# Moving the apply step of Q and K, and half of the V casts, in a fused transformer layer

## The chip, the cores and the metric

The kernel runs on the 8 cores of one Trainium2 chip. Each core computes one of the eight sequences of the batch (2048 tokens, 1024 features) on its own; the cores exchange nothing. The metric is the device time of the slowest core in microseconds.

## What is computed

One layer: a layer norm, then the sum of the input, an attention block with its own MLP, and a mixture of eight experts. The change touches the projections of Q, K and V and the normalisation of Q and K per head. Cut to that:

```python
xn = _rms_norm(x, ln1_w)                       # x: [B, 2048, 1024]
q = (xn @ Wq).reshape(B, S, HEADS, HEAD_DIM)   # 16 heads of 64
k = (xn @ Wk).reshape(B, S, HEADS, HEAD_DIM)
v = (xn @ Wv).reshape(B, S, HEADS, HEAD_DIM)
q = _normalize_kq(q)     # kq * rsqrt(sum(kq^2 over the head) + 1e-6)
k = _normalize_kq(k)
...
attn = softmax(causal(scale * (q @ k^T + bias)))
y = attn @ v @ Wo + x ; MLP(rms_norm(y)) + y
```

## The kernel before

The kernel works feature-major: a tile holds 128 features (two heads) on the partitions and all T = 2048 tokens in the free dimension, so NP = T // 512 = 4 pieces of 512 columns, and NTT = T // 128 = 16 tiles of tokens. There are eight feature tiles, counted by d. The stages are: layer norm and transposes, gating, experts (to about 790 us), RMS norm and the Wq projections (to about 867 us), the Wk projections with the normalisation of Q, the Wv projections with the normalisation of K, attention, Wo, and the MLP.

Instructions are written by hand with the helper `kb.op(engine, fn, reads, writes)`. Each engine runs its own in the order in which they are written. The helper derives semaphore waits from the names in `reads` and `writes`: a reader waits for the last writer of the name, a writer for the last writer and all readers since. A name stands for a whole tile (or PSUM bank `pb0` to `pb7`), never for a part of it; for an engine's semaphore the wait is for its count at the last such instruction.

The parts that matter here:

- `proj_unit` (L744 to 773): a unit of 8 x 4 = 32 matmuls (L755) into banks 0 to 3, then four casts on VectorE (L770) to the Q or K tile. It first issues the eight loads of the next weight tile from POOL.
- `qn_sq` (L775): the square of a Q or K tile on VectorE, 128 x 2048 (L778).
- `qn_stats` (L782 to 805): for each of four pieces a matmul that sums the squares per head (L787), then Ln and Exp on ScalarE (L792, L796) through one scratch row, and for Q a multiply by the scale on VectorE (L801). The result is `rowb16`, one name per parity of d.
- `qn_apply_piece` (L807 to 818): a matmul that spreads one piece of `rowb16` over 128 partitions (L810), and a multiply on VectorE into the Q or K tile (L815).
- `v_transpose` (L834 to 845): a transpose of 128 x 128 of V on TensorE into bank 4 (L837), and two casts of 64 columns each out of the bank into `VtL` (L843), one for each head. Both casts write the name `vtl{tt}`, and the next transpose writes the name `pb4`, which both read.

The loop over d for Wk (L823 to 830) writes: square of Q d, projection of K d, statistics of Q d, apply of Q d-1. The apply of Q 7 follows (L831). The loop for Wv (L847 to 875) writes: square of K d, loads, for each k of 0 to 7 four projection matmuls (L858), two transposes of V d-1 and, at odd k, one apply piece of K d-1 in bank 7, then four copies of V d (L872) and the statistics of K d. Sixteen transposes of V 7 and four apply pieces of K 7 end the stretch (L876 to 879).

Of the kernel before, what the change touches and what calls it, by code (L numbers as in the profile page):

```python
# [194 lines left out]
def build_nc(T=2048):  # L195
    nc = bass.Bass("TRN2", target_bir_lowering=False)
    NTT = T // 128
    NP = T // 512
# [15 lines left out]
    kb = KB(nc)  # L214
# [6 lines left out]
    pb = [None] * 8  # L221
# [36 lines left out]
    def ld(dst, src, cast=False, sem=MISC, reads=(), writes=(), silent=False,  # L258
# [15 lines left out]
       writes=("ln1b",))  # L274
    ld(ln2b[:, :], A(w_d["ln2"], 0, [[D, 1], [1, D]]), cast=True, sem="qC",
       writes=("ln2b",))
    for e_ in range(NTRU):
        ld(ebCol[:, e_ * 8:(e_ + 1) * 8], A(w_d["eb"], e_ * D, [[1, 128], [128, 8]]),
           writes=("ebCol",), slow=True)

    G, V, S, TE = "gpsimd", "vector", "scalar", "tensor"
# [462 lines left out]
    def proj_unit(wname, dst, dkey, dout, nxt):  # L744
        def go():
            par = dout % 2
            if nxt is not None:
                wload(1 - par, w_d[nxt[0]], 0, nxt[1] * 128,
                      (nxt[1] + 1) * 128, f"wst{1 - par}")
            pbase = (dout % 2) * 2 if NP <= 2 else 0  # L750
            for k in range(8):
                for pp in range(NP):
                    bk = pbase + pp if NP <= 2 else pp
                    kb.op(TE, lambda e, par=par, k=k, pp=pp, bk=bk:
                          e.matmul(pb[bk][:, 0:512],  # L755
                                   Wst[par][:, k * 128:(k + 1) * 128],
                                   XN2[k][:, pp * 512:(pp + 1) * 512],
                                   start=(k == 0), stop=(k == 7)),
                          reads=(f"wst{par}", f"y16p_{k}"),
                          writes=(f"pb{bk}",), inc=(k == 7))  # L760
            for pp in range(NP):
                bk = (pbase + pp) if NP <= 2 else pp
                if dst is None:
                    kb.op(V, lambda e, pp=pp, bk=bk:
                          e.tensor_copy(Vf32[:, pp * 512:(pp + 1) * 512],
                                        pb[bk][:, 0:512]),
                          reads=(f"pb{bk}",), writes=("vf32",))
                else:
                    kb.op(V, lambda e, dout=dout, pp=pp, bk=bk:
                          e.tensor_copy(dst[dout][:, pp * 512:(pp + 1) * 512],  # L770
                                        pb[bk][:, 0:512]),
                          reads=(f"pb{bk}",), writes=(dkey.format(dout),))
        return go
# [8 lines left out]
    def qn_stats(XB, keyfmt, c, fold_scale, bank0):  # L782
        pr = c % 2
        for pp in range(NP):
            bk = bank0 + pp % 2
            kb.op(TE, lambda e, pr=pr, pp=pp, bk=bk:
                  e.matmul(pb[bk][0:2, 0:512], selq[:, :],  # L787
                           sqP[pr][:, pp * 512:(pp + 1) * 512],
                           start=True, stop=True),
                  reads=(f"sq{pr}", "selq"), writes=(f"pb{bk}",))  # L790
            kb.op(S, lambda e, bk=bk:
                  e.activation(rowscrP[0:2, :], pb[bk][0:2, 0:512], AF.Ln,  # L792
                               bias=epsc[0:2, 2:3]),
                  reads=(f"pb{bk}", "epsc"), writes=("rowscrP",))
            kb.op(S, lambda e, pr=pr, pp=pp:
                  e.activation(rowb16[pr][0:2, pp * 512:(pp + 1) * 512],  # L796
                               rowscrP[0:2, :], AF.Exp, scale=-0.5),
                  reads=("rowscrP",), writes=(f"rowb16_{pr}",))
            if fold_scale:
                kb.op(V, lambda e, c=c, pr=pr, pp=pp:  # L800
                      e.tensor_scalar(rowb16[pr][0:2, pp * 512:(pp + 1) * 512],  # L801
                                      rowb16[pr][0:2, pp * 512:(pp + 1) * 512],
                                      scaleP[:, c:c + 1], None, ALU.mult),
                      reads=(f"rowb16_{pr}", "scaleP"),
                      writes=(f"rowb16_{pr}",))
# [17 lines left out]
    for d in range(8):  # L823
        nxt = ("Wk", d + 1) if d < 7 else ("Wv", 0)
        qn_sq(Q16, "q16_{}", d)
        proj_unit("Wk", K16, "k16_{}", d, nxt)()
        qn_stats(Q16, "q16_{}", d, True, 4)
        if d > 0:
            for pp in range(NP):
                qn_apply_piece(Q16, "q16_{}", d - 1, pp, 6 + pp % 2)  # L830
    for pp in range(NP):  # L831
        qn_apply_piece(Q16, "q16_{}", 7, pp, 6 + pp % 2)

    def v_transpose(c, tt):  # L834
        reg = (tt % 4) * 128
        kb.op(TE, lambda e, tt=tt, reg=reg:
              e.transpose(pb[4][:, reg:reg + 128],  # L837
                          Vf32[:, tt * 128:(tt + 1) * 128], iden_f[:, :]),
              reads=("vf32", "iden_f"), writes=("pb4",))
        for hf, eng in ((0, V), (1, V)):  # L840
            hh = 2 * c + hf
            kb.op(eng, lambda e, tt=tt, reg=reg, hf=hf, hh=hh:
                  e.tensor_copy(VtL[tt][:, hh * 65:hh * 65 + 64],  # L843
                                pb[4][:, reg + hf * 64:reg + hf * 64 + 64]),
                  reads=("pb4",), writes=(f"vtl{tt}",))

    for d in range(8):  # L847
        par = d % 2
        qn_sq(K16, "k16_{}", d)
        if d < 7:  # L850
            wload(1 - par, w_d["Wv"], 0, (d + 1) * 128, (d + 2) * 128,
                  f"wst{1 - par}")
        pbase = (d % 2) * 2 if NP <= 2 else 0
        for k in range(8):
            for pp in range(NP):
                bk = pbase + pp if NP <= 2 else pp
                kb.op(TE, lambda e, par=par, k=k, pp=pp, bk=bk:
                      e.matmul(pb[bk][:, 0:512],  # L858
                               Wst[par][:, k * 128:(k + 1) * 128],
                               XN2[k][:, pp * 512:(pp + 1) * 512],  # L860
                               start=(k == 0), stop=(k == 7)),
                      reads=(f"wst{par}", f"y16p_{k}"),
                      writes=(f"pb{bk}",), inc=(k == 7))
            if d > 0 and 2 * k < NTT:
                v_transpose(d - 1, 2 * k)
                v_transpose(d - 1, 2 * k + 1)
            if d > 0 and k % 2 == 1 and (k - 1) // 2 < NP:
                qn_apply_piece(K16, "k16_{}", d - 1, (k - 1) // 2, 7)
        for pp in range(NP):
            bk = pbase + pp if NP <= 2 else pp  # L870
            kb.op(V, lambda e, pp=pp, bk=bk:
                  e.tensor_copy(Vf32[:, pp * 512:(pp + 1) * 512],  # L872
                                pb[bk][:, 0:512]),
                  reads=(f"pb{bk}",), writes=("vf32",))
        qn_stats(K16, "k16_{}", d, False, 5)
# [462 lines left out]
```

## Time and profile before

| | us |
|---|---|
| median of 3 runs (2912.61 to 2984.51) | 2916.29 |
| the profiled execution | 2929.51 |
| its span on the slowest core, number 2 | 2927.9 |
| spans of the eight cores | 2897.7 to 2927.9 |
| TensorE busy | 2174.8 (74%) |
| VectorE busy | 1037.4 (35%) |
| ScalarE busy | 605.7 (21%) |
| GpSimd busy | 660.4 (23%) |

The span runs from the first to the last instruction of a core; the execution's own time has 1.6 us around it. Busy shares are averages over all stages. Matmuls overlap each other, so the duration of one is longer than its share of a dense stream: a 512-column matmul in such a stream starts about 0.22 us after the one before it when the granted clock is 2.4 GHz and about 0.43 us when it is 1.2 GHz. The mean granted clock over the execution is 0.765 of full.

### The profile page before, as it was taken

Reading aid. Unit: us, or ns where it says so; the run is one execution under the profiler, and the core shown is the slowest. Engines: PE = TensorE matmul, PEld = TensorE weight load, DVE = VectorE, ACT = ScalarE, POOL = GpSimd, SP = SyncE. Lnnn points to the kernel's source line nnn. Section 1 sums busy time; section 2 is a strip of 40 time slices with the busy share of each in tenths; the row PEclk is TensorE's granted clock in tenths of the full one; section 3 lists DMA queues with packets and bytes.
Section 4 is the critical chain, followed back from the end, with each engine's and each line's share of the span. In section 5 each row is a group of like instructions: output and inputs, shape, how many; then the busy total and the mean of one; then the engine's idle time right before and its main releaser. Section 6 shows DMA issues by size and latency. Waiting matters only on the chain.

```text
span 2927.9 us, 28314 instructions; the slowest of 8 cores (2897.7 to 2927.9 us)
## 1 busy us (share of the span) xinstructions
PE 2174.8 (74%) x7379; PEld 745.0 (25%) x7379; DVE 1037.4 (35%) x2125; ACT 605.7 (21%) x1204; POOL 660.4 (23%) x764
## 2 busy tenths in 40 slices
PE   2457999998686677768889898865369989988322
PEld 0212444443132222212222222221013323332111
DVE  3725444443434444445555555532320000000111
ACT  1400000000003211126665666610002101210000
POOL 0021478776142211000000000013135302410000
PEclk9987999999597755555655655667569999999655
DMA  2202323233121100001100111025168513421343
GB/s 42 80 1 29 44 29 44 29 44 121 19 27 17 14 8 8 4 15 19 19 15 11 19 19 19 12 62 129 72 92 112 91 48 68 54 47 58 105 130 124
DMA packets 137150, 139.20 MB, mean 48 GB/s; under 512 B 46320, under 2 KB 116976, under 8 KB 133882
## 3 DMA queue, kind: packets, MB, share of 16 engines
q0 software_dynamic: 96320, 61.39, 16.2%
q1 hardware_dynamic: 40682, 76.00, 8.2%
q8 instruction: 73, 1.20, 0.2%
q14 instruction: 75, 0.61, 0.1%
HBM read 160.80 MB, written 33.69 MB: 66 GB/s over the span
## 4 chain that ended last, share of the span: by engine, by line
PE 64%; DVE 10%; issue 9%; DMA 8%; ACT 5%; POOL 2%; SPq 1%; DVEq 1%; ACTq 0%; POOLq 0%
PE pb L627 8%; PE pb L1199 8%; PE pb L973 7%; PE s L1029 7%; PE pb L755 4%; PE pb L858 4%; DMA asl<-accscr 3%; PE pb4b L1218 3%; DMA accw<-accscr 2%; PE pb7b L1218 2%; PE pb5b L627 2%; PE pb4b L627 2%; PE pb6b L627 2%; PE pb7b L627 2%; ACT pt L1036 2%
## 5 line engine op out<-in xcount | busy, mean ns | idle before, releaser
L1036 ACT ACTIVATE pt<-s 128x512 bf16<-128x512 f32 (+3 forms) x640 | 306.8, 533 | 270.5 <-PE s L1029 243.4
L1040 DVE TENSOR_TENSOR pt<-pt,tst 128x512 bf16<-128x512 bf16 (+3 forms) x640 | 238.3, 383 | 247.5 <-ACT pt L1036 233.4
L660 POOL TENSOR_TENSOR acc<-acc,mtmp 128x2048 f32<-128x2048 f32 x56 | 253.6, 4529 | 102.9 <-DVE mtmp L650 102.9
L1029 PE MATMUL s<-q,k 64*128 64x512 bf16 (+3 forms) x640 | 272.1, 525 | 0.9 <-ACT pt L1036 0.2
L973 PE MATMUL pb<-pt,vtl 128*65 128x512 bf16 (+3 forms) x640 | 262.3, 528 | 10.0 <-DVE pt L1040 0.4
L1199 PE MATMUL pb<-k,ws 128*128 128x512 bf16 x1024 | 241.3, 384 | 31.7 <-DMA ws<-W 22.2
L627 PE MATMUL pb<-xn,we 128*128 128x512 bf16 x1024 | 233.4, 381 | 5.2 <-DVE cwb L600 0.4
L264 POOL DMA_DIRECT2D ws<-W x264 | 139.9, 572 | 324.1 <-PE pb L1199 260.9
L1240 DVE TENSOR_TENSOR acw<-acw,pb4b 128x512 f32<-128x512 f32 x8 | 5.5, 689 | 559.8 <-PE pb7b L1218 379.5
L1199 PEld LDWEIGHTS pb<-k,ws 128*128 128x128 bf16 x1024 | 100.7, 99 | 173.1 <-issue 69.1
L264 POOL DMA_DIRECT2D tst<-cscr x16 | 8.6, 540 | 603.0 <-DVE pt L1040 507.4
L1297 PE MATMUL pb6b<-iden_f,asl 128*128 128x128 f32 x64 | 28.6, 447 | 148.0 <-DMA asl<-accscr 128.4
L755 PE MATMUL pb<-y16p,wst 128*128 128x512 bf16 x480 | 127.8, 417 | 12.7 <-DVE q L770 9.9
L627 PEld LDWEIGHTS pb<-xn,we 128*128 128x128 bf16 x1024 | 98.3, 98 | 135.3 <-issue 23.2
L1209 ACT ACTIVATE h<-pb 128x512 bf16<-128x512 f32 x96 | 57.3, 597 | 345.7 <-PE pb L1199 293.1
L650 DVE SCALAR_TENSOR_TENSOR mtmp<-pb,ebCol,cwb 128x512 f32<-128x512 f32 x112 | 84.1, 751 | 117.4 <-PE pb L627 108.6
L973 PEld LDWEIGHTS pb<-pt,vtl 128*65 128x65 bf16 x640 | 80.7, 148 | 150.2 <-issue 143.3
L858 PE MATMUL pb<-y16p,wst 128*128 128x512 bf16 x256 | 113.5, 599 | 0.1
L710 ACT ACTIVATE rowscrP<-pb4b,epsc 1x512 f32<-1x512 f32 x1 | 0.7, 677 | 535.0 <-PE pb6b L704 535.0
L843 DVE CAST vtl<-pb4b 128x64 bf16<-128x64 f32 x256 | 57.9, 226 | 142.7 <-PE pb4b L837 129.1
L1029 PEld LDWEIGHTS s<-q,k 64*128 64x128 bf16 x640 | 52.8, 107 | 207.1 <-issue 203.8
L837 PE MATMUL pb4b<-iden_f,vf 128*128 128x128 f32 x128 | 55.1, 431 | 65.8 <-DVE vtl L843 65.7
(263 smaller groups left out, 2877.7 us busy)
## 6 DMA issues: line engine op xcount, KB each, us to landing
ws<-W POOLq DMA_DIRECT2D x264, 64.0 KB, 2.6
we<-ew POOLq DMA_DIRECT2D x128, 128.0 KB, 5.4
xt<-x SPq DMA_DIRECT2D x16, 512.0 KB, 3.5
accscr<-acc SPq DMA_DIRECT2D x8, 1024.0 KB, 3.8
tst<-cscr POOLq DMA_DIRECT2D x16, 512.0 KB, 5.5
accw<-accscr SPq DMA_DIRECT2D x8, 1024.0 KB, 8.0
accscr<-accw SPq DMA_DIRECT2D x8, 1024.0 KB, 5.0
acw<-accscr SPq DMA_DIRECT2D x16, 512.0 KB, 5.0
```

Of the source, the lines that this page charges most:

```text
L264: e.dma_start(d, s, allow_slow_non_contiguous=sl),
L627: e.matmul(pb[bk][:, 0:512], We16[par][:, k * 512 + col: k * 512 + col + 128], XN16[k][:, pp * 512:(pp + 1) * 512], start=(k == 0), stop=( ...
L650: e.scalar_tensor_tensor(mtmp[mp][:, pp * 512:(pp + 1) * 512], pb[bk][:, 0:512], ebCol[:, e_ * 8 + dout:e_ * 8 + dout + 1], cwbA[e_][:, pp ...
L660: e.tensor_tensor(ACC[dout][:, :], ACC[dout][:, :], mtmp[mp][:, :], ALU.add),
L755: e.matmul(pb[bk][:, 0:512], Wst[par][:, k * 128:(k + 1) * 128], XN2[k][:, pp * 512:(pp + 1) * 512], start=(k == 0), stop=(k == 7)),
L858: e.matmul(pb[bk][:, 0:512], Wst[par][:, k * 128:(k + 1) * 128], XN2[k][:, pp * 512:(pp + 1) * 512], start=(k == 0), stop=(k == 7)),
L973: e.matmul(pb[b][0:65, q % 512:q % 512 + w], VtL[kt][:, h * 65:(h + 1) * 65], Pt[pslot][:, j0:j0 + w], start=(kt == 0), stop=lb),
L1029: e.matmul(s16[sbk][:, 0:w], K16[c][po:po + 64, kt * 128:(kt + 1) * 128], Q16[c][po:po + 64, q:q + w], start=True, stop=True),
L1036: e.activation(Pt[pslot][:, jc:jc + w2], s16[sbk][:, 0:w2], AF.Exp),
L1040: e.tensor_tensor(Pt[pslot][:, jc:jc + w2], Pt[pslot][:, jc:jc + w2], Tst[par][:, jc:jc + w2], ALU.mult),
L1199: e.matmul(pb[pbase + pc][:, 0:512], Wst1[par][:, k * 256 + hl * 128: k * 256 + hl * 128 + 128], YN16[k][:, t0c + pc * 512: t0c + (pc + 1) ...
L1218: e.matmul(pb[bk][:, 0:512], W2R[:, hk * D + dout * 128: hk * D + (dout + 1) * 128], H16[hk][:, pc * 512:(pc + 1) * 512], start=(hk == 0), ...
```

## The change

Three edits. In the Wk loop the apply of Q d-1 is written ahead of the projection of K d instead of behind the statistics of Q d. In `v_transpose` the second cast becomes a copy on ScalarE; both still write `vtl{tt}`. In the Wv loop the apply pieces of K d-1 go to k = 0, 1, 2, 3 instead of k = 1, 3, 5, 7.

```diff
     for d in range(8):
         nxt = ("Wk", d + 1) if d < 7 else ("Wv", 0)
         qn_sq(Q16, "q16_{}", d)
-        proj_unit("Wk", K16, "k16_{}", d, nxt)()
-        qn_stats(Q16, "q16_{}", d, True, 4)
         if d > 0:
             for pp in range(NP):
                 qn_apply_piece(Q16, "q16_{}", d - 1, pp, 6 + pp % 2)
+        proj_unit("Wk", K16, "k16_{}", d, nxt)()
+        qn_stats(Q16, "q16_{}", d, True, 4)
     for pp in range(NP):
         qn_apply_piece(Q16, "q16_{}", 7, pp, 6 + pp % 2)
...
-        for hf, eng in ((0, V), (1, V)):
+        for hf in range(2):
             hh = 2 * c + hf
-            kb.op(eng, lambda e, tt=tt, reg=reg, hf=hf, hh=hh:
-                  e.tensor_copy(VtL[tt][:, hh * 65:hh * 65 + 64],
-                                pb[4][:, reg + hf * 64:reg + hf * 64 + 64]),
-                  reads=("pb4",), writes=(f"vtl{tt}",))
+            if hf == 0:
+                kb.op(V, lambda e, tt=tt, reg=reg, hh=hh:
+                      e.tensor_copy(VtL[tt][:, hh * 65:hh * 65 + 64],
+                                    pb[4][:, reg:reg + 64]),
+                      reads=("pb4",), writes=(f"vtl{tt}",))
+            else:
+                kb.op(S, lambda e, tt=tt, reg=reg, hh=hh:
+                      e.copy(VtL[tt][:, hh * 65:hh * 65 + 64],
+                             pb[4][:, reg + 64:reg + 128]),
+                      reads=("pb4",), writes=(f"vtl{tt}",))
...
-            if d > 0 and k % 2 == 1 and (k - 1) // 2 < NP:
-                qn_apply_piece(K16, "k16_{}", d - 1, (k - 1) // 2, 7)
+            if d > 0 and k < NP:
+                qn_apply_piece(K16, "k16_{}", d - 1, k, 7)
```

## Rows read from the trace of the kernel before

**Rows 1.** Page, part 4: the chain that ended last, by engine.
```profile
PE 64%; DVE 10%; issue 9%; DMA 8%; ACT 5%; POOL 2%; SPq 1%; DVEq 1%; ACTq 0%; POOLq 0%
```
**Rows 2.** Windows, Wv stretch: length, busy of PE, PEld, DVE, ACT, POOL, clock, DMA, GB/s.
```profile
1010.40:1248.10 237.70, 173.52 (x429) 56.02 (x429) 100.73 (x294) 39.17 (x60) 25.41 (x48) 0.53 0.07 7
```
**Rows 3.** Timeline, Wk units 0 and 1: start, duration, engine, line, operation [idle before].
```profile
877.71 0.38 PE L787 MATMUL pb5b<-sq,selq 128*2 128x512 bf16 x1 [1.11 <-ACT rowscrP L792]
878.02 7.39 PE L755 MATMUL pb<-y16p,wst 128*128 128x512 bf16 x32
...
885.34 0.38 PE L787 MATMUL pb4b<-sq,selq 128*2 128x512 bf16 x1
```
**Rows 4.** Timeline, from the statistics of unit 1 to those of unit 2.
```profile
888.18 0.38 PE L787 MATMUL pb5b<-sq,selq 128*2 128x512 bf16 x1 [1.11 <-ACT rowscrP L792]
...
892.01 0.34 DVE L801 TENSOR_SCALAR rowb<-rowb,scaleP 2x512 bf16<-2x512 bf16 x1 [1.21 <-ACT rowb L796]
892.28 0.67 DVE L815 TENSOR_TENSOR q<-q,pb6b 128x512 bf16<-128x512 bf16 x1
...
893.20 0.58 PE L810 MATMUL pb6b<-rowb,sel2T 2*128 2x512 bf16 x1 [4.11 <-DVE q L815]
...
894.58 7.98 PE L755 MATMUL pb<-y16p,wst 128*128 128x512 bf16 x29
...
895.45 1.22 DVE L778 TENSOR_TENSOR sq<-q 128x2048 bf16<-128x2048 bf16 x1
...
903.44 0.38 PE L787 MATMUL pb4b<-sq,selq 128*2 128x512 bf16 x1
```
**Rows 5.** Timeline, unit 7 of Wk and the start of Wv.
```profile
987.70 10.15 PE L755 MATMUL pb<-y16p,wst 128*128 128x512 bf16 x32
...
997.77 0.38 PE L787 MATMUL pb4b<-sq,selq 128*2 128x512 bf16 x1
...
1000.62 0.38 PE L787 MATMUL pb5b<-sq,selq 128*2 128x512 bf16 x1 [1.11 <-ACT rowscrP L792]
...
1010.45 9.03 PE L858 MATMUL pb<-y16p,wst 128*128 128x512 bf16 x32
```
**Rows 6.** Timeline, two k steps of a Wv unit, the first with an apply piece.
```profile
1059.37 0.45 PE L837 MATMUL pb4b<-iden_f,vf 128*128 128x128 f32 x1 [0.91 <-DVE vtl L843]
...
1060.28 1.89 PE L858 MATMUL pb<-y16p,wst 128*128 128x512 bf16 x4
...
1061.96 0.42 PE L837 MATMUL pb4b<-iden_f,vf 128*128 128x128 f32 x1
1062.49 0.55 DVE L843 CAST vtl<-pb4b 128x64 bf16<-128x64 f32 x2 [1.34 <-PE pb4b L837]
...
1063.29 0.45 PE L837 MATMUL pb4b<-iden_f,vf 128*128 128x128 f32 x1 [0.91 <-DVE vtl L843]
...
1063.53 1.91 PE L858 MATMUL pb<-y16p,wst 128*128 128x512 bf16 x4
```
**Rows 7.** Timeline of the first stage: hand-overs between ScalarE, TensorE and VectorE.
```profile
59.97 0.27 ACT L424 COPY xnf<-pb6b 128x128 f32<-128x128 f32 x1 [0.45 <-PE pb6b L420]
...
60.38 0.45 PE L420 MATMUL pb6b<-iden_f,xnt 128*128 128x128 f32 x1 [0.27 <-ACT xnf L424]
...
62.02 0.21 DVE L399 TENSOR_SCALAR st_s<-st_s 128x1 f32<-128x1 f32 x1
62.33 0.29 ACT L404 ACTIVATE st_s<-st_s,epsc 128x1 f32<-128x1 f32 x1 [0.91 <-DVE st_s L399]
```
**Rows 8.** Timeline, start of a Wv unit: ScalarE's last step and T2.
```profile
1087.91 0.63 ACT L796 ACTIVATE rowb<-rowscrP 2x512 bf16<-2x512 f32 x1
...
1088.51 0.45 PE L837 MATMUL pb4b<-iden_f,vf 128*128 128x128 f32 x1 [0.92 <-DVE vtl L843]
```
**Rows 9.** Timeline, start of the tail of sixteen transposes: the second one, and ScalarE.
```profile
1249.46 0.45 PE L837 MATMUL pb4b<-iden_f,vf 128*128 128x128 f32 x1 [0.91 <-DVE vtl L843]
...
1250.37 0.63 ACT L796 ACTIVATE rowb<-rowscrP 2x512 bf16<-2x512 f32 x1
```

## Prediction of the time after the change

> **What bounds the kernel now.** I read the page first. The chain of work that ended last is TensorE for 64% and VectorE for 10% [rows 1], so time is won or lost where TensorE waits. The edits lie between about 867 and 1277 us: the Wk projections with the normalisation of Q, then the Wv projections with the transposes of V and the normalisation of K. The windows view shows the second stretch: 237.70 us, TensorE busy for 173.52, ScalarE for only 39.17, at a mean granted clock of 0.53, which is almost wholly the 1.2 GHz level [rows 2]. So one engine is full but slow, ScalarE has room, and every step is short. Then I read the timeline around one unit of each kind, looking for what released TensorE.
>
> In the Wk stretch a unit is 32 matmuls, then four statistics matmuls paced by ScalarE, then four pieces of "apply". Unit 1 follows unit 0's statistics at once: last statistics matmul at 877.71, projection from 878.02 to the next statistics at 885.34, so a gap of 0.31 and 7.32 us of projection at 2.4 GHz [rows 3]. From unit 2 on the apply of the unit before stands in between: last statistics matmul 888.18, next projection 894.58, a gap of 6.40 [rows 4]. There are six such gaps, 6.38 to 6.42 each. TensorE is idle there for 4.11 us until VectorE has finished its multiply at 892.28, and that multiply stands behind the last L801 at 892.01, although its own data are long ready: the queue, not the data, makes it late. TensorE comes out of the gap at 1.2 GHz. Unit 2 needs 903.44 - 894.58 = 8.86 us, unit 7 needs 997.77 - 987.70 = 10.07 [rows 4, 5]; these are the first and last of six that alternate between about 8.9 and 10.0, so the mean is 9.47. After the last unit two rounds of apply follow each other: 1000.62 to 1010.45, a gap of 9.83 [rows 5].
>
> In the Wv stretch each of eight k steps is four matmuls (1060.28 to 1061.96, 1.68 us, 0.42 each, the 1.2 GHz level), a transpose T1, two casts one after the other on VectorE, and a transpose T2 that must wait for both: 1061.96 to 1063.29, 1.33 us. T2 to the next matmuls is 0.24 us without an apply piece and 1060.28 - 1059.37 = 0.91 with one [rows 6].
>
> **The change, part by part.**
>
> *Apply moved ahead of the projection.* In each of d = 1 to 7 the apply of d-1 now follows that unit's own statistics directly. Those data are not ready yet. Its first matmul reads rowb16, whose last writer is the fourth L801, ending at 892.01 + 0.34 = 892.35. VectorE to TensorE takes 893.20 - (892.28 + 0.67) = 0.25, so the matmul would start at 892.60 and, at 1.2 GHz (0.58, as at 893.20), be readable near 893.28. In VectorE's queue the square of Q (L778, 1.22 us) now stands in front of the multiplies: 892.28 + 1.22 less the overlap of 0.05 gives 893.45. The later of the two, 893.45, replaces 892.28: every following step is 1.17 later, and the gap becomes 6.40 + 1.17 = 7.57 [rows 4]. Behind the last unit there is no square and only one round: 6.40 + 1.00 = 7.40.
> Before: 0.31 + 6 x 6.40 + 9.83 = 48.5 us. After: 7 x 7.57 + 7.40 = 60.4. That is +11.9.
> Unit 1 loses its seamless start, so it should be paced like the others: 9.47 - 7.32 = +2.15. Sum for the stretch: +14.0. No transfer is issued in another order, since each weight load of POOL waits for the projection before it and takes its place as before.
>
> *Half of each V cast on ScalarE.* Both copies name the same tile vtl as written, so the ScalarE copy waits for the VectorE cast as well as for the transpose. They run one after the other as before, not side by side. The new chain is T1 to the cast 0.53, the cast 0.23, the hand-over to ScalarE 62.33 - (62.02 + 0.21) = 0.10, the copy, and ScalarE to TensorE 60.38 - (59.97 + 0.27) = 0.14 [rows 6, 7]. No row has a 64-column copy. The bound above is the 128-column one, 0.27. Below, ScalarE's Exp over 512 columns takes 0.63 [rows 8] against 0.27 for 128 [rows 7], 0.36 / 384 = 0.94 ns a column, so 0.27 - 0.06 = 0.21; that is the form nearest to it and I take it. The chain is 0.53 + 0.23 + 0.10 + 0.21 + 0.14 = 1.21 against 1.33: 0.12 less. If both hand-overs took the 0.25 of VectorE to TensorE and the copy 0.27 it would be 1.53: 0.20 more. I take 1.21, since two of the three parts are rows of the very same engines.
> The ScalarE page of the Trainium skill ("ScalarE: Activation LUTs", What ACT_TABLE_LOAD costs) gives 186 ns plus 0.833 ns a column with immediate scale and bias, 293 ns for 128 columns, where the trace has 0.27 us; for 64 columns it would say 239 ns and the gain would be 0.09 a step instead of 0.12, about 2 us in all.
>
> *What ScalarE has queued in front.* At the start of a Wv unit ScalarE still works on K's statistics: its last step ends at 1087.91 + 0.63 = 1088.54. The first copy of a unit waits for it, so T2 comes at 1088.54 + 0.21 + 0.14 = 1088.89 instead of 1088.51: +0.38 [rows 8].
>
> *K's pieces at k = 0 to 3 instead of 1, 3, 5, 7.* Each costs 0.91 - 0.24 = 0.67 in its place. The one that leaves k = 7 was followed by the statistics, 0.13 cheaper. The piece at k = 0 needs rowb16, complete at 1088.54, before T2: no new stall. In exchange the copies of V out of the banks are free some 0.6 earlier, which nobody waits for.
>
> Each of seven units: 7 x (-0.12) + 0.38 + 0.13 = -0.33, so -2.3. In the tail sixteen transposes run as a bare chain. The second now waits until ScalarE is free at 1250.37 + 0.63 = 1251.00, and starts at 1251.35, not 1249.46: +1.9 [rows 9]. Fourteen more steps at -0.12 give -1.7. The tail is +0.2.
>
> **Sum.** 14.0 - 2.3 + 0.2 = +11.9 us. Against the profiled execution's 2929.5 that is 2941.4; the median of the runs shown is 13.2 lower, 2916.3, and there the forecast is 2928.2. Whatever lies behind 1277 us is shifted and not changed.
>
> **The rivals.**
>
> *A, slower than before by over 2%: the hand-overs are dear.* Place: T1, cast, copy, T2, 56 times in the loop and 15 times in the tail. With the upper bound of 1.53 the loop and the tail cost 71 x 0.32 = 23 us more than forecast, 2951. To pass 2% (58 us above 2916, so 46 above the forecast) each chain must take 0.65 more, 1.86 in all. For it: the copy waits for TensorE and VectorE, and the next transpose for VectorE and ScalarE, two waits where there was one. Against it: no hand-over in the rows is above 0.25.
> The trace page of the Trainium skill ("Perfetto Trace Analysis", Identifying Dependency Chains) says that an instruction which waits on several engines may get extra semaphore instructions put in front of it, which speaks for A; no row of before shows what such an instruction costs here.
>
> *B, the clock stays at 1.2 GHz through the Wk units.* The gap of 7.57 has only four short matmuls in it. At 0.42 a unit takes 13.4 instead of 9.47: 7 x 3.9, and 4.4 for the first Wv unit, which now takes about 9.0 [rows 5]: +32, 2960. Against it: TensorE is dense for 32 matmuls, and after gaps of 6.40 and of 9.83 the level came back each time.
>
> *C, the Wv steps gain the 2.4 GHz level.* Steps 4 to 7 have no pieces now: four in a row of 1.68 + 1.21 + 0.24 = 3.1 us, with nothing between the steps. At 7.32 / 32 = 0.23 a matmul, a step is 0.76 shorter; over 28 steps 21 us, 2907. It puts the kernel ahead of before from 16 such steps on. Against it: the loop fell to 1.2 GHz and stayed there, though half of its steps had no piece either, and its mean was 0.53 [rows 2].
>
> *D, the moved apply does not cool TensorE,* because the gap is cut up in another way than before: the 2.15 of each of seven units comes back, -15 against the forecast, 2913. Against it: the idle part of the gap is as long as before, 888.56 to 892.60.
>
> **How the numbers follow.** Forecast 0.70, A 0.08 (of which 0.02 past 2%), B 0.07, C 0.08, D 0.07. The forecast is that of the first. Its own range is 2920 to 2940, from the unit pace (7.32 to 10.07 for unit 1) and the copy. To hold 8 in 10 with the upper bound of A, I take 2913 to 2950. A measurement tells 2% from no change here, 58 us; only the far end of A reaches it, with 0.02, and 0.01 more for A and B together; on the other side none of the cases does, and 0.01 is left for C with more steps than priced: slower 0.03, faster 0.01, same 0.96.
>
> **What the profile after would show.** Right: seven gaps near 7.6 from last statistics to projection, one near 7.4; L778 between the last L801 and the first L815 of a unit; unit 1 taking 8.9 to 10.0; T1 to T2 near 1.21 in the loop and in the tail; the ScalarE copy starting only after the VectorE cast has ended, and the first of a unit after K's last Exp; the granted clock of the Wv stretch still near 0.5. Wrong: a copy beside the cast, a chain above 1.4, a Wv stretch with a clock clearly above 0.53, or a Wk unit of 13 us.

## The result, and the profile after

The changed kernel takes 2944.0 us (median of 10 runs), the kernel before 2919.2 (median of 10, with the three shown above). The ratio is 1.0084, 95% interval 1.0071 to 1.0096: +0.84%, +24.5 us. The forecast was 2928.2, +11.9. So the sign, the verdict (within 2%) and the range of 2913 to 2950 held; the forecast case's own range, 2920 to 2940, did not, and the size was about half of what came.

The profiled execution of after took 2942.17 us, its slowest core 2940.6, again number 2. Some executions of either kernel run with one die at a lower clock; the ratios leave them out.

The whole of the difference has to be found between the first statistics matmul of unit 0 and the first matmul of attention, since nothing else was edited. Read from the timelines of all cores (core 2; the others agree within 0.4, except core 5, which has 137.1 and 150.7 in the first line and 265.8 before in the second):

| stretch | before | after | forecast |
|---|---|---|---|
| Wk: first statistics matmul to first Wv projection | 135.6 | 153.7 | +14.0 |
| Wv: to the first matmul after the last memset | 266.6 | 269.6 | -2.1 |
| sums of V and first tile of the bias, to attention | 19.6 | 20.7 | 0 |
| together | 421.8 | 444.0 | +11.9 |

That is +22.2 of the 24.5 us. The other 2 us are not located: attention (638.3 to 650.9 us on the eight cores before, 639.2 to 649.5 after), Wo (197.1 to 216.1 and 197.6 to 203.9) and the MLP (766.4 to 769.9 and 767.1 to 774.7) scatter by more than that.

The chain that ended last looks as before: TensorE 64% and VectorE 10% as in [rows 1], ScalarE 6% where it had 5%.

Timeline of after, from the last statistics matmul of unit 0 to the first of unit 1, to be laid beside [rows 3, 4]:
```profile
876.24 0.38 PE L787 MATMUL pb5b<-sq,selq 128*2 128x512 bf16 x1 [1.12 <-ACT rowscrP L792]
...
880.06 0.34 DVE L801 TENSOR_SCALAR rowb<-rowb,scaleP 2x512 bf16<-2x512 bf16 x1 [1.20 <-ACT rowb L796]
880.33 1.21 DVE L778 TENSOR_TENSOR sq<-q 128x2048 bf16<-128x2048 bf16 x1
...
880.55 0.58 PE L810 MATMUL pb6b<-rowb,sel2T 2*128 2x512 bf16 x1 [3.94 <-DVE rowb L801]
...
881.47 0.67 DVE L815 TENSOR_TENSOR q<-q,pb6b 128x512 bf16<-128x512 bf16 x1
...
883.76 10.19 PE L755 MATMUL pb<-y16p,wst 128*128 128x512 bf16 x32
...
893.88 0.38 PE L787 MATMUL pb4b<-sq,selq 128*2 128x512 bf16 x1
```
The order is the forecast one: last L801, square, multiply. TensorE waits 3.94 us for `rowb16`; the gap is 883.76 - 876.24 = 7.52 us where unit 1 had 0.31; and the projection behind it takes 893.88 - 883.76 = 10.12 us where it took 7.32. Seven gaps are 7.52 to 7.56, the last is 7.45. What had not been forecast stands in the next column of this table, the projection times:

| unit | 1 | 2 | 3 | 4 | 5 | 6 | 7 | first Wv |
|---|---|---|---|---|---|---|---|---|
| gap before | 0.31 | 6.40 | 6.42 | 6.39 | 6.39 | 6.38 | 6.39 | 9.83 |
| projection before | 7.32 | 8.86 | 10.03 | 8.80 | 10.02 | 8.94 | 10.07 | 8.96 |
| gap after | 7.52 | 7.53 | 7.56 | 7.53 | 7.53 | 7.52 | 7.52 | 7.45 |
| projection after | 10.12 | 10.11 | 10.09 | 9.97 | 10.04 | 10.08 | 10.09 | 10.14 |

The alternation is gone and all units have the slow value. That holds for seven of the eight cores. On core 5, behind gaps of the same 7.53 to 7.55, the seven projections take 8.62, 9.36, 9.72, 9.77, 9.94, 10.02 and 10.07: they start fast and drift to the slow value.

In the Wv stretch, after's windows view has this line, for [rows 2] (here the whole stretch; over its own whole stretch, before has VectorE busy for 111.83, ScalarE for 41.78 and a clock of 0.53):
```profile
1027.10:1296.70 269.60, 185.97 (x449) 59.63 (x449) 83.19 (x218) 68.11 (x192) 25.41 (x48) 0.52 0.07 6
```
ScalarE rose from 41.78 to 68.11 us busy, VectorE fell from 111.83 to 83.19, the clock stayed. Two chains T1, cast, copy, T2 of the timeline follow, the first from unit 1, the second from unit 2, for [rows 6]; L844 is the cast, L849 the copy:
```profile
1046.45 0.42 PE L837 MATMUL pb4b<-iden_f,vf 128*128 128x128 f32 x1
...
1046.98 0.23 DVE L844 CAST vtl<-pb4b 128x64 bf16<-128x64 f32 x1 [1.34 <-PE pb4b L837]
...
1047.29 0.22 ACT L849 CAST vtl<-pb4b 128x64 bf16<-128x64 f32 x1 [2.35 <-DVE vtl L844]
...
1047.65 0.45 PE L837 MATMUL pb4b<-iden_f,vf 128*128 128x128 f32 x1 [0.78 <-ACT vtl L849]
...
1078.29 0.42 PE L837 MATMUL pb4b<-iden_f,vf 128*128 128x128 f32 x1
1078.89 0.23 DVE L844 CAST vtl<-pb4b 128x64 bf16<-128x64 f32 x1 [1.41 <-PE pb4b L837]
1079.20 0.21 ACT L849 CAST vtl<-pb4b 128x64 bf16<-128x64 f32 x1 [2.35 <-DVE vtl L844]
...
1079.56 0.45 PE L837 MATMUL pb4b<-iden_f,vf 128*128 128x128 f32 x1 [0.85 <-ACT vtl L849]
```
The copy starts 0.31 behind the cast in both, never beside it. But the cast starts 0.53 behind T1 in unit 1 and 0.60 in unit 2, so T1 to T2 is 1.20 there and 1.27 here. It is 1.27 in nearly every step of the units from 2 on behind the first, and 1.29 to 1.30 in the tail, where before has 1.36. The first step of a unit and of the tail shows the queue on ScalarE, for [rows 8, 9]:
```profile
1074.83 0.63 ACT L796 ACTIVATE rowb<-rowscrP 2x512 bf16<-2x512 f32 x1
1075.37 0.19 ACT L849 CAST vtl<-pb4b 128x64 bf16<-128x64 f32 x1
...
1075.69 0.45 PE L837 MATMUL pb4b<-iden_f,vf 128*128 128x128 f32 x1 [1.18 <-ACT vtl L849]
...
1267.19 0.45 PE L837 MATMUL pb4b<-iden_f,vf 128*128 128x128 f32 x1
...
1269.57 0.63 ACT L796 ACTIVATE rowb<-rowscrP 2x512 bf16<-2x512 f32 x1
...
1270.44 0.45 PE L837 MATMUL pb4b<-iden_f,vf 128*128 128x128 f32 x1 [2.80 <-ACT vtl L849]
```

### The profile page after: what moved, and what is told of

Same layout as the page of the kernel before. It is cut to its first block, busy times and chain, and to the rows that moved or that the text cites. A ratio compares the mean times of both kernels' runs of the same rounds, so it can differ in the third digit from the quotient of the medians.

```text
span 2940.6 us, 28695 instructions; the slowest of 8 cores (2923.8 to 2940.6 us)
## 1 busy us (share of the span) xinstructions
PE 2198.5 (75%) x7379; PEld 749.6 (25%) x7379; DVE 1008.7 (34%) x1997; ACT 632.1 (21%) x1332; POOL 660.4 (22%) x764
## 4 chain that ended last, share of the span: by engine, by line
PE 64%; DVE 10%; issue 9%; DMA 7%; ACT 6%; POOL 2%; DVEq 1%; SPq 1%; ACTq 0%; POOLq 0%
PE pb L627 8%; PE pb L1205 8%; PE pb L979 7%; PE s L1035 7%; PE pb L755 4%; PE pb L864 4%; DMA asl<-accscr 3%; PE pb4b L1224 3%; PE pb7b L1224 2%; PE pb5b L627 2%; PE pb4b L627 2%; PE pb5b L1224 2%; PE pb6b L1224 2%; ACT pt L1042 2%; PE pb7b L627 2%
## 5 line engine op out<-in xcount | busy, mean ns | idle before, releaser
L755 PE MATMUL pb<-y16p,wst 128*128 128x512 bf16 x480 | 134.3, 433 | 12.7 <-DVE q L770 9.9
L864 PE MATMUL pb<-y16p,wst 128*128 128x512 bf16 x256 | 115.4, 607 | 0.1
L627 PE MATMUL pb5b<-xn,we 128*128 128x512 bf16 x256 | 97.0, 379 | 4.8
```

The source lines that it names most:

```text
L627: e.matmul(pb[bk][:, 0:512], We16[par][:, k * 512 + col: k * 512 + col + 128], XN16[k][:, pp * 512:(pp + 1) * 512], start=(k == 0), stop=( ...
L755: e.matmul(pb[bk][:, 0:512], Wst[par][:, k * 128:(k + 1) * 128], XN2[k][:, pp * 512:(pp + 1) * 512], start=(k == 0), stop=(k == 7)),
L864: e.matmul(pb[bk][:, 0:512], Wst[par][:, k * 128:(k + 1) * 128], XN2[k][:, pp * 512:(pp + 1) * 512], start=(k == 0), stop=(k == 7)),
```

## Experiments

Three questions: do the three edits account for the time one by one; why did all projections take the slow value; and what holds the cast back by 0.07 us. Then: what would have been the better move. Ratios are against the kernel before, on the same chip. "Wk" and "Wv" are the stretches of the table above.

### The edits one by one

`wk_only` is the first hunk of the change on the kernel before.

```diff
+        if d > 0:
+            for pp in range(NP):
+                qn_apply_piece(Q16, "q16_{}", d - 1, pp, 6 + pp % 2)
         proj_unit("Wk", K16, "k16_{}", d, nxt)()
         qn_stats(Q16, "q16_{}", d, True, 4)
-        if d > 0:
-            for pp in range(NP):
-                qn_apply_piece(Q16, "q16_{}", d - 1, pp, 6 + pp % 2)
```

> Only the move of Q's apply ahead of the projection; V casts and K's pieces as in the kernel before. The changed kernel takes 153.6 us from the first statistics matmul of unit 0 to the first Wv projection against 135.5 before. If the parts add up, this kernel has the same 153.6 (+18.1), seven gaps of 7.52, every projection of units 1 to 7 about 10.1, and the first Wv projection 10.1 instead of 8.95. In all +18 to +21 us, ratio about 1.0065. If instead most of the +24.5 comes from the cast on ScalarE, this one shows less than +12.

Measured: ratio 1.0081 (1.0048 to 1.0113). Wk 153.5 to 154.1 on six cores and 150.7 on two, Wv 265.5 to 266.0, the rest 19.5 or 19.6 on seven cores and 20.9 on one. The parts nearly add up: by the ratio this edit alone is the whole loss, by the stretches +17.5 of the +22.2, and the theory that the ScalarE cast costs most of it is out. On core 2 six of the seven gaps are 7.52 and one reads 7.96, with a projection of 9.70 behind it; the first Wv projection reads 9.74, behind a gap of 7.86. Both are no finding: the trace has 31 of these units' 32 matmuls, so the first record is missing, and gap and projection together are 17.66 and 17.60, as 7.56 + 10.10 and 7.46 + 10.14 on the cores that have all 32. What does differ is the two cores with 150.7: their gaps are 7.52 to 7.56 too, and their projections go from 8.6 to 10.07 as on core 5 of the changed kernel.

`copy_only` is the second hunk alone.

```diff
-        for hf, eng in ((0, V), (1, V)):
+        for hf in range(2):
...
+            else:
+                kb.op(S, lambda e, tt=tt, reg=reg, hh=hh:
+                      e.copy(VtL[tt][:, hh * 65:hh * 65 + 64],
+                             pb[4][:, reg + 64:reg + 128]),
+                      reads=("pb4",), writes=(f"vtl{tt}",))
```

> Only the second V cast on ScalarE. By the trace of the changed kernel: T1 to T2 1.20 where no copy has written the tile before (unit 1), 1.27 from unit 2 on against 1.33; unit 1 loses 1.4 at its first step, because ScalarE is still busy with K's statistics, the later units 0.26 each; the tail loses 1.9 at its first step and wins 0.07 at each of 14 more. In all 0 to +3 us, ratio 1.000 to 1.001. The theory that the hand-overs to ScalarE are what the change costs wants +10 or more here.

Measured: ratio 1.0002 (0.9983 to 1.0021). Wv 266.4 to 267.0 on seven cores and 269.0 on one, where before has 265.8 to 266.6; Wk as before. As expected, nothing: what the chain wins per step it loses to ScalarE's queue at the start of each unit.

`kpiece_only` is the third hunk alone.

```diff
-            if d > 0 and k % 2 == 1 and (k - 1) // 2 < NP:
-                qn_apply_piece(K16, "k16_{}", d - 1, (k - 1) // 2, 7)
+            if d > 0 and k < NP:
+                qn_apply_piece(K16, "k16_{}", d - 1, k, 7)
```

> Only K's apply pieces at k = 0 to 3. The work is the same, in another place: a piece costs 0.91 - 0.24 = 0.67 wherever transposes stand in front of it and projection matmuls behind it, and 0.53 at k = 7, in front of the statistics. So +0.14 to +0.2 for each of seven units, +1.2 us, ratio 1.0004. The theory that four steps without a piece bring the 2.4 GHz level back wants a Wv stretch shorter by 5 us or more and a granted clock above 0.53.

Measured: ratio 1.0007 (0.9992 to 1.0021). On the four cores whose Wk stretch is that of before (135.2 to 136.0) Wv is 267.7 to 268.1, about +1.6, and the rest 20.4, +0.8. The other four took 144.6 to 145.9 in Wk, which this edit does not touch, and are left out. No sign of the higher clock level (0.53 over Wv); a little dearer than nothing, as expected.

The three together: in us of the stretches +17.5, -0.1 and +2.4, about 20, against +22.2 for all at once. The missing 2 are not located.

### Why every projection took 10.1 us

Two theories. L: the slow phase behind a gap grows with the gap. P: the level of 2.4 GHz returns at moments that this loop does not set; a projection is slow until the next such moment, and because a later start is then followed by a shorter projection, the units fall into step with them.

`sq_behind` makes the gap shorter. In the changed kernel:

```diff
-        qn_sq(Q16, "q16_{}", d)
         if d > 0:
             for pp in range(NP):
                 qn_apply_piece(Q16, "q16_{}", d - 1, pp, 6 + pp % 2)
+        qn_sq(Q16, "q16_{}", d)
```

> The changed kernel with the square of Q written behind the apply pieces. The first multiply then waits only for its matmul, some 0.2 us earlier, so the gap is 7.3 instead of 7.52. Theory L (the slow phase of a projection grows with the gap in front of it): projection 10.1 or a little less, the period of a unit falls from 20.48 to 20.3, -1.5 us in all. Theory P (the granted level returns at moments that the loop does not set, and the units fall in step with them): the projection gets longer by what the gap gets shorter, 10.3, and the period stays 20.48: 0 us in all, ratio against before still 1.008.

Measured: ratio 1.0066 (1.0043 to 1.0089). The gap is 7.31 or 7.32 and the projections of units 1 to 6 on core 2 are 10.21, 10.27, 9.88, 10.15, 10.24, 10.28 (the 9.88 stands behind a gap that reads 7.75: its first matmul has no record, and the cores that have it show 7.35 and 10.26 to 10.28). They are longer by 0.09 in unit 1 and by 0.2 in unit 6, so the later ones by all that the gap is shorter, as P has it. The period from unit 1 to unit 7 is (1004.54 - 881.84) / 6 = 20.45 us, against (1006.69 - 883.76) / 6 = 20.49 in the changed kernel. The seventh projection then took only 8.61: there the units fell out of step, which P as I had written it did not say, and which makes Wk 152.2 instead of 153.7. Six cores did so in this unit (151.6 to 152.2); one started out of step (150.5) and one never fell out (153.4). The time alone could not have told L from P: L had expected -1.5 us.

`sq_twice` makes the gap longer, by a second square of Q.

```diff
         qn_sq(Q16, "q16_{}", d)
+        if d > 0:
+            qn_sq(Q16, "q16_{}", d)
```

> The changed kernel with the square of Q done twice, so that each of the seven gaps gets 1.22 us of VectorE work more, 8.74 instead of 7.52, with the same matmuls. Theory L (the slow phase grows with the gap): projection 10.1 or more, period 21.6, Wk stretch +8.5 us, ratio against before 1.011. Theory P (the level returns at moments that the loop does not set): the projection starts 1.22 later, meets the same moment, runs a smaller part of its matmuls at 1.2 GHz and takes 8.9; the period stays near 20.4 and the 1.22 us cost nothing: ratio still 1.008.

Measured: ratio 1.0048 (1.0018 to 1.0079). The timeline of core 2 around the gap before unit 6:
```profile
976.96 0.38 PE L787 MATMUL pb5b<-sq,selq 128*2 128x512 bf16 x1 [1.11 <-ACT rowscrP L792]
...
981.06 2.54 DVE L778 TENSOR_TENSOR sq<-q 128x2048 bf16<-128x2048 bf16 x2
...
985.82 8.84 PE L755 MATMUL pb<-y16p,wst 128*128 128x512 bf16 x32
...
994.58 0.38 PE L787 MATMUL pb4b<-sq,selq 128*2 128x512 bf16 x1
```
The gap is 985.82 - 976.96 = 8.86, 1.33 longer, and the projection 994.58 - 985.82 = 8.76, 1.3 shorter. Along the units the projections go 9.44, 9.11, 8.93, 8.72, 8.76, 8.76, 8.77 and the periods 21.14, 20.85, 20.91, 20.41, 20.46, 20.46: they settle on the same period of about 20.45 us. Seven gaps got 9.3 us more of waiting between them, and Wk grew by 1.2 (153.7 to 154.9). L would have had +8.5. L has fallen and P stands, in both directions. Core 5 of the changed kernel says it without any edit: equal gaps, projections from 8.62 to 10.07.

The traces also show when the level comes back. In the kernel before, windows laid along units 2 to 4 of core 2 give (columns as in [rows 2]; the third number from the end is the granted clock):
```profile
890.95:897.70 6.75, 4.22 (x10) 1.36 (x11) 4.14 (x6) 0.81 (x2) 0.00 (x0) 0.50 0.05 5
897.80:907.95 10.15, 7.37 (x31) 2.54 (x29) 3.35 (x6) 3.40 (x6) 1.28 (x3) 1.00 0.03 3
908.05:918.20 10.15, 6.59 (x15) 2.09 (x16) 4.51 (x7) 1.72 (x3) 2.86 (x6) 0.50 0.25 23
918.25:928.40 10.15, 6.22 (x26) 2.03 (x24) 3.62 (x7) 4.19 (x7) 4.25 (x8) 1.00 0.25 25
928.50:935.25 6.75, 4.09 (x10) 1.27 (x11) 4.14 (x6) 0.93 (x2) 0.00 (x0) 0.50 0.04 5
935.35:945.50 10.15, 7.43 (x32) 2.54 (x30) 3.36 (x6) 3.35 (x6) 3.83 (x8) 1.00 0.17 16
```
The level comes back at 897.8, 918.2 and 935.3, and further on at 955.8, 972.8 and 993.3: 20.5 and 17.1 us apart in turn, while the projections start 18.0 to 18.2 and 19.2 to 19.5 apart. So each second one starts further ahead of the moment and runs longer at 1.2 GHz (13 matmuls of 32 instead of 7 or 8), and this is the alternation. In the changed kernel the moments are all 20.5 apart, and every projection from unit 2 on has about 13 slow matmuls; in `sq_twice` they are 20.5 apart too, and the settled units have 7. In `sq_behind` the last step, before the projection of 8.61, is 17.1. No step in the Wk units of core 2 lies between in these four traces: the moments do not follow the loop by fractions. What sets the moments is not shown.

### What holds the cast back

From unit 2 on the V tile was last written by a ScalarE copy, for the heads before. So the cast has a second semaphore wait, for ScalarE, whose value was reached some 30 us earlier.

`two_names` takes that wait away, by a name for each half; the copy still waits for the cast.

```diff
                       e.tensor_copy(VtL[tt][:, hh * 65:hh * 65 + 64],
                                     pb[4][:, reg:reg + 64]),
-                      reads=("pb4",), writes=(f"vtl{tt}",))
+                      reads=("pb4",), writes=(f"vtlA{tt}",))
...
                       e.copy(VtL[tt][:, hh * 65:hh * 65 + 64],
                              pb[4][:, reg + 64:reg + 128]),
-                      reads=("pb4",), writes=(f"vtl{tt}",))
+                      reads=("pb4",), writes=(f"vtlB{tt}",),
+                      extra_waits=(("V", kb.cnt["V"]),))
```

> The changed kernel with one name for the VectorE half and one for the ScalarE half of a V tile. The copy still waits for the cast (by an explicit wait), so the two never read the bank together, but the cast no longer waits for the ScalarE copy that wrote the same tile for the heads before. If that second, long satisfied wait is what moved the cast from 0.53 to 0.60 us behind T1, it is 0.53 in every unit, T1 to T2 is 1.20 throughout, and 57 chains give -4 us: Wv stretch 265.6 instead of 269.6, ratio 1.007. If the 0.07 has another cause, nothing changes.

Measured: Wv 269.2 to 269.6, as if nothing had been done (ratio 1.0036, 1.0006 to 1.0066). By the time my explanation had fallen. The timeline says otherwise: the cast starts at 0.53 behind T1 in all units, as expected, but the copy now starts 0.37 behind the cast instead of 0.31, and T1 to T2 is 1.25 to 1.26. The edit had put the copy's explicit wait for VectorE in front of its wait for the transpose; before, it stood behind it. So the 0.06 had moved from the cast to the copy. That made the question sharper: does the satisfied wait cost its time only where it stands behind the one that ends last?

`wait_order` keeps every wait of the changed kernel and turns round the two of the cast.

```diff
+                old = (kb.bufs.get(f"vtl{tt}") or {}).get("w")
                 kb.op(V, lambda e, tt=tt, reg=reg, hh=hh:
...
-                      reads=("pb4",), writes=(f"vtl{tt}",))
+                      reads=("pb4",), writes=(f"vtl{tt}",),
+                      extra_waits=(old,) if old else ())
```

> The changed kernel with the same waits, but the VectorE cast waits first for the old ScalarE copy of its tile (long done) and then for the transpose, instead of the other way round. In the changed kernel the cast starts 0.53 us behind T1 in unit 1, where no copy has written the tile, and 0.60 from unit 2 on. Theory: a satisfied wait that is written behind the one that ends last costs its own 0.06 to 0.07 us on the path, one written in front of it costs nothing. Then the cast is at 0.53 and T1 to T2 1.20 in all units, and the Wv stretch 265.6 us instead of 269.6 (57 chains of 0.07). If the wait costs 0.07 wherever it is written, 269.6 stays.

Measured: Wv 265.4 to 266.0 on all cores, -3.8 us against 269.6; ratio 1.0055 (1.0033 to 1.0078) where the changed kernel has 1.0084 (1.0071 to 1.0096). The intervals touch, and `two_names` has 1.0036 with nothing gained, so it is the stretch that shows the gain and not the ratio. A chain of unit 2 (core 2; L845 cast, L851 copy):
```profile
1079.71 0.42 PE L837 MATMUL pb4b<-iden_f,vf 128*128 128x128 f32 x1
1080.24 0.22 DVE L845 CAST vtl<-pb4b 128x64 bf16<-128x64 f32 x1 [1.34 <-PE pb4b L837]
1080.55 0.21 ACT L851 CAST vtl<-pb4b 128x64 bf16<-128x64 f32 x1 [2.35 <-DVE vtl L845]
...
1080.91 0.45 PE L837 MATMUL pb4b<-iden_f,vf 128*128 128x128 f32 x1 [0.78 <-ACT vtl L851]
```
0.53, 0.31, T1 to T2 1.20, the forecast chain of 1.21, now in every unit (1.22 in the tail). The trace has a semaphore instruction for each wait. In the changed kernel VectorE's for TensorE stands at 1078.75, its one for ScalarE at 1078.82, and the cast at 1078.89; here the one for TensorE is at 1080.17 and the cast at 1080.24, because the one for ScalarE had run before T1 began. The same waits in another order are worth 4 us here.

### A better move

`mid_apply`: in the kernel before, the apply pieces of Q d-1 go between the projection matmuls of unit d, after k = 4 to 7, where `rowb16` should be ready; the projection calls `mid(k - 4)` behind the matmuls of k, and Q 7 is done so in the first Wv unit.

```diff
-        proj_unit("Wk", K16, "k16_{}", d, nxt)()
-        qn_stats(Q16, "q16_{}", d, True, 4)
-        if d > 0:
-            for pp in range(NP):
-                qn_apply_piece(Q16, "q16_{}", d - 1, pp, 6 + pp % 2)
+        mid = None if d == 0 else (lambda pp, d=d: qn_apply_piece(
+            Q16, "q16_{}", d - 1, pp, 6 + pp % 2))
+        proj_unit("Wk", K16, "k16_{}", d, nxt, mid)()
+        qn_stats(Q16, "q16_{}", d, True, 4)
```

> The kernel before, with the apply pieces of Q d-1 between the projection matmuls of unit d, after k = 4 to 7 (those of Q 7 in the first Wv unit). The projection then follows the statistics after 0.31 us, as unit 1 does in the kernel before, and TensorE never waits for a multiply. If the gap and the cold start behind it are the cost of the Wk stretch, a unit takes 0.31 + 7.32 + 0.9 for four more matmuls + 2.85 = 11.4 instead of 18.9 and the stretch 83 instead of 135.5 us: -50 to -55 us, ratio 0.982. If VectorE's queue (square, multiplies, four casts) becomes the bound, a unit is above 13 us.

Measured: ratio 0.9869 (0.9813 to 0.9925), 2888.6 us. Wk is 98.6 to 100.7 instead of 135.6, but 83 had been expected, and Wv with its four more pieces is 270.1 on most cores. From unit 2 on a unit takes 13.5 to 14.6 us, not 11.4. Three things add up. The first is the price of a piece (core 4; L812 is the apply matmul):
```profile
879.72 0.38 PE L755 MATMUL pb<-y16p,wst 128*128 128x512 bf16 x1
880.03 0.39 PE L812 MATMUL pb7b<-rowb,sel2T 2*128 2x512 bf16 x1
880.56 1.02 PE L755 MATMUL pb<-y16p,wst 128*128 128x512 bf16 x4
```
The piece costs 880.56 - 879.72 = 0.84 us from the matmul before it to the one behind it, where two projection matmuls are 0.22 apart: 0.62 for a piece, not 0.22. In the trace a semaphore instruction of TensorE, for TensorE's own semaphore, stands behind the apply matmul at 880.45; the apply matmul ends at 880.42, and the projection matmul starts only at 880.56. So the helper has the projection wait for the end of the apply matmul. No run leaves this wait out.

The second is `rowb16`, which is not always ready. In unit 5 TensorE waits 0.70 us for it, because the statistics are late: ScalarE is idle for 1.51 us before the Exp of the second piece (L798) until VectorE has done the multiply of the first (L803), which stands in VectorE's queue behind casts of K (L772):
```profile
927.90 1.49 DVE L772 CAST k<-pb 128x512 bf16<-128x512 f32 x2
...
929.31 0.35 DVE L803 TENSOR_SCALAR rowb<-rowb,scaleP 2x512 bf16<-2x512 bf16 x1
929.75 0.63 ACT L798 ACTIVATE rowb<-rowscrP 2x512 bf16<-2x512 f32 x1 [1.51 <-DVE rowb L803]
...
934.06 0.37 PE L812 MATMUL pb6b<-rowb,sel2T 2*128 2x512 bf16 x1 [0.70 <-DVE rowb L803]
```
So VectorE's order does bear on a unit, as the expectation had named for a unit above 13 us. The third is the clock, which over the Wk stretch of this core is 0.91 and not 1.00:
```profile
875.00:973.70 98.70, 81.39 (x295) 26.95 (x294) 55.09 (x92) 38.07 (x59) 30.46 (x58) 0.91 0.22 21
```
Unit 5, with the wait and at 2.4 GHz throughout, has a projection of 10.14 us; those with a 1.2 GHz phase from unit 2 on have 10.43 to 10.90.

`one_cast`: in the kernel before, one VectorE cast of 128 columns for both heads.

```diff
-        for hf, eng in ((0, V), (1, V)):
...
+        kb.op(V, lambda e, tt=tt, reg=reg:
+              e.tensor_copy(A(VtL[tt], 2 * c * 65, [[H * 65, 128], [65, 2], [1, 64]]),
+                            A(pb[4], reg, [[512, 128], [64, 2], [1, 64]])),
+              reads=("pb4",), writes=(f"vtl{tt}",))
```

> The kernel before with one VectorE cast of 128 columns for both heads in place of two of 64, still in bank 4. T1 to T2 is 0.53 + 0.29 + 0.25 = 1.07 instead of 1.33 in 56 steps and 15 times 0.27 less in the tail: -18 to -19 us, Wv stretch 248, ratio 0.9935. If the clock returns in part of the stretch, more.

Measured: ratio 0.9883 (0.9840 to 0.9927). Wv is 229.5 to 229.9 on all cores, 36.6 less, twice what the chain gives: the first units now keep the 2.4 GHz level, and the mean clock of the stretch is 0.61 instead of 0.53. Its windows line, core 2, shows a clock of 1.00 (in shares of full) in a piece of the stretch, where the kernel before is at 1.2 GHz from 1027.5 on:
```profile
1012.00:1040.00 28.00, 18.70 (x80) 7.27 (x79) 13.52 (x29) 7.68 (x12) 8.31 (x16) 1.00 0.17 17
```

`two_banks`: the same, with the transposes in turn in banks 4 and 7, so that T2 doesn't wait for T1's cast, and K's pieces at k = 0 to 3 in bank 6 (the last four, behind the tail, in turn in banks 5 and 6).

```diff
+        vb = 4 + 3 * (tt % 2)
-              e.transpose(pb[4][:, reg:reg + 128],
+              e.transpose(pb[vb][:, reg:reg + 128],
...
+                qn_apply_piece(K16, "k16_{}", d - 1, k, 6)
```

> The kernel before with only the Wv part of both_better: one cast for both heads, transposes in turn in banks 4 and 7, K's pieces at k = 0 to 3 in bank 6; the Wk part as before. both_better had 153.5 to 157.3 us for the Wv stretch with four pieces of Q in it. If the two parts add up: Wk stretch 135.5 as before, Wv stretch 152 to 156, -112 us in all, ratio 0.961.

Measured: ratio 0.9595 (0.9553 to 0.9638). Wk 135.4 to 136.0, Wv 152.7 to 154.5: -112 to -114 us, as expected.

`both_better` is the edits of `mid_apply` and of `two_banks` together, with no other line changed.

> mid_apply, and in the Wv stretch one VectorE cast of 128 columns for both heads, transposes in turn in banks 4 and 7, K's pieces at k = 0 to 3 in bank 6. T2 no longer waits for T1's casts: T1 to T2 0.24 instead of 1.33, at 56 places -61 us, and the tail of sixteen about half, -10. Together with mid_apply -120 to -130 us, ratio 0.957. If the denser Wv stretch also gets the 2.4 GHz level, up to 40 us more, ratio 0.943.

Measured: 2770.2 us, ratio 0.9447 (0.9400 to 0.9495). Wk 98.6 to 98.8, Wv 157.3 on six cores and 153.5 on two. From the timeline, the two transposes and the first cast of a step (core 4; L836 transposes, L840 cast):
```profile
1007.55 0.42 PE L836 MATMUL pb4b<-iden_f,vf 128*128 128x128 f32 x1
...
1007.76 0.42 PE L836 MATMUL pb7b<-iden_f,vf 128*128 128x128 f32 x1
1008.08 0.29 DVE L840 CAST vtl<-pb4b 128x128 bf16<-128x128 f32 x1 [1.34 <-PE pb4b L836]
```
The windows line of the Wv stretch of the same core:
```profile
969.20:1122.70 153.50, 118.64 (x453) 47.41 (x452) 89.20 (x225) 45.03 (x69) 26.80 (x51) 0.83 0.13 12
```
T1 to T2 is 0.21 us here (0.11 in most steps), and the clock over the stretch is 0.83 instead of 0.53; over the Wk stretch it is 0.91 instead of 0.79. Both gains go with TensorE stopping less.

## Why the prediction was right, and where it was not

**Direction, and which edit carries it: right.** The moved apply was priced at +14.0, the rest at -2.1; alone they measured +17.5 and about +2, so the sign of the rest was wrong.

**Gap: right.** Forecast 7.57 and 7.40, measured 7.52 to 7.56 and 7.45. The step that carried it was to read the last writer of `rowb16` and VectorE's queue, not the place of the edit.

**Unit pace: mis-sized.** The mean of six alternating values, 9.47 (from the first and the last; all six give 9.45), was taken over into the new loop for unit 1 only, and the other six were left as they were. In its place all seven took 10.0 to 10.1 on core 2: unit 1 +2.8 instead of +2.15, units 2 to 7 +0.6 each, 3.7 us for the six, and the first Wv projection 10.14 instead of 8.96, +1.2. The reading that failed is that the slow phase is a property of the gap. It is a matter of when the projection starts against the moment at which the level returns, and an alternation between two values was the hint: equal gaps, 6.38 to 6.42, gave 8.9 and 10.0 in turn.

**The chain of the copy: right to 0.01 in its parts, off by 0.07 from unit 2 on.** Forecast 1.21; measured 1.20 in unit 1, 1.27 later, 1.29 to 1.30 in the tail. Not counted was that the cast gets a second wait through the name `vtl`, because the last writer is now another engine. 56 chains of 0.07 (seven in each of units 2 to 7, fourteen in the tail) are 4 us, as `wait_order` shows with 3.8. The Trainium skill ("Perfetto Trace Analysis", Identifying Dependency Chains) says that an instruction which waits on several engines may get extra semaphore instructions in front of it. The trace of after agrees in so far as two of them stand in front of the cast, written by the helper; such a wait costs 0.06 to 0.07 us where it stands last. The figure for ACTIVATE in the Trainium skill ("ScalarE: Activation LUTs", What ACT_TABLE_LOAD costs) gave an estimate of 0.24 us for the 64-column copy; the trace has 0.21 to 0.22, and 0.19 for the first of a unit.

**ScalarE's queue in front of the copy: right, and twice incomplete.** +0.38 was forecast for T2 of a unit, measured 1.60 against 1.34, +0.26, in five of the units from 2 on, and 1.88 in unit 3; the tail's first step +1.9, measured 3.25 against 1.36, +1.89. But unit 1 runs at 2.4 GHz, gets to T1 sooner and waits longer: its first step is 1043.86 - 1041.24 = 2.62 us against about 1.2 before. That instance stood in the trace and was priced like the others.

**K's pieces: right.** +0.13 a unit forecast; alone they measured about +1.6 for seven, on the four cores that can be read.

**Not forecast: +1.1 behind the stretch.** The first group of sums of V ran longer at 1.2 GHz (6.45 us for sixteen matmuls against 5.10). "Shifted and not changed" does not hold for the first matmuls behind a change. `wait_order` has 19.4 there on six cores and 20.8 on two. On the six the matmuls pass from 0.43 to 0.22 us apart after the seventh, on the two after the fifteenth: it goes with the moment at which the level returns, here too.

**The rivals.** A fell: no chain above 1.33, but for the first of each unit and of the tail, which waits for ScalarE's queue, and one of 1.55. The upper bound of the range, 2950, came from A; that 2944.0 fell under it is luck, since what filled the room was the unit pace, the second wait and the stretch behind. B fell: the level came back in every unit. C fell for this change (clock 0.52), but its mechanism is real: with a chain of 0.92 to 1.07 (`one_cast`) the clock over the Wv stretch is 0.61, with one of 0.11 to 0.21 (`two_banks`) 0.83. D fell: no unit was spared, and even the fastest unit 1, on core 5, took 8.62 and not 7.32.

## What to carry to other kernels

Before moving work "into a gap", find the last writer of what it reads and what stands in its engine's queue: here the gap was the wait for that writer, and the move put it into one more unit. Work goes between matmuls that don't depend on it, not between their groups; and shortening a chain that stops TensorE (one cast for two, a second bank) beat sharing it out over two engines here (229.9 and 153 us against 266.9). Where a helper derives waits from names, a second engine writing the same name adds a wait to the first; write the wait that ends last behind all others.

## What the runs showed that I had not expected

- A slow phase can soak up delay. Seven gaps longer by 1.33 us each cost 1.2 us in all, and shorter gaps gave almost nothing in six of seven units: the mean period stayed at about 20.45 us.
- The 8.9 and 10.0 us in turn of six equal units came from the moments at which the 2.4 GHz level returned, 20.5 and 17.1 us apart in turn.
- A semaphore wait that has long been met costs 0.06 to 0.07 us on VectorE and on ScalarE when it stands behind the wait that ends last, and nothing measurable in front of it.
- An apply matmul between projection matmuls costs 0.62 us more than none, at 2.4 GHz, where a projection matmul costs 0.22; the trace shows the next matmul waiting for TensorE's own semaphore.
- A cast of 128 columns takes 0.29 us on VectorE where one of 64 takes 0.23.
